# Attention layers of a graph-transformer kernel: head products from half-precision parts stacked over the partitions, squared lengths from token-major rows

## The reference

```python
def softmax_kernel(data, proj, is_query, eps=0.0001):
    d = data.shape[-1]
    normalizer = d ** (-0.25)
    ratio = proj.shape[0] ** (-0.5)
    data_dash = jnp.einsum('bhnd,md->bhnm', data * normalizer, proj)
    diag = jnp.sum(data ** 2, axis=-1, keepdims=True) * 0.5 * normalizer ** 2
    if is_query:
        m = jnp.max(data_dash, axis=-1, keepdims=True)
    else:
        m = jnp.max(data_dash, axis=(-2, -1), keepdims=True)
    return ratio * (jnp.exp(data_dash - diag - m) + eps)
...
for i in range(DEPTH):                      # DEPTH = 2
    y = layernorm(x, ln1_g[i], ln1_b[i])
    q = (y @ Wq[i] + bq[i]).reshape(B, N, HEADS, DIM_HEAD).transpose(0, 2, 1, 3)
    k = (y @ Wk[i] + bk[i]).reshape(B, N, HEADS, DIM_HEAD).transpose(0, 2, 1, 3)
    v = (y @ Wv[i] + bv[i]).reshape(B, N, HEADS, DIM_HEAD).transpose(0, 2, 1, 3)
    qp = softmax_kernel(q, proj[i], True)
    kp = softmax_kernel(k, proj[i], False)
    k_sum = kp.sum(axis=2)
    d_inv = 1.0 / jnp.einsum('bhnm,bhm->bhn', qp, k_sum)
    ctx = jnp.einsum('bhnm,bhnd->bhmd', kp, v)
    o = jnp.einsum('bhmd,bhnm,bhn->bhnd', ctx, qp, d_inv)
    x = x + o.transpose(0, 2, 1, 3).reshape(B, N, INNER) @ Wo[i] + bo[i]
    y = layernorm(x, ln2_g[i], ln2_b[i])
    x = x + gelu(y @ W1[i] + b1[i]) @ W2[i] + b2[i]
```

## Time and profile before

| what | value |
|---|---|
| three runs | 3261.3, 3269.97 and 3289.47 us; median 3269.97 |
| profiled execution | span 3276.7 us; no other time of it is given |
| TensorE busy | 2823.4 us (86%) |
| VectorE busy | 1606.1 us (49%) |
| ScalarE busy | 1067.3 us (33%) |
| GpSimd busy | 1172.1 us (36%) |
| TensorE's mean granted clock | 0.911 of full speed |

### The profile page before, as it was taken

One profiled execution on the slowest core, in us unless ns is written; L12 is line 12 of the kernel. 1 busy time (PEld: TensorE's weight loads), 2 busy tenths in 40 slices (PEclk: granted clock), 3 DMA queues, 4 the chain that ended last, 5 costly groups with the idle time before them and its releaser, 6 DMA issues. The chain is left out here.

```text
span 3276.7 us, 45967 instructions
## 1 busy us (share of the span) xinstructions
PE 2823.4 (86%) x16963; PEld 1813.0 (55%) x16963; DVE 1606.1 (49%) x3306; ACT 1067.3 (33%) x2420; POOL 1172.1 (36%) x1445
## 2 busy tenths in 40 slices
PE   7897999899899989979995974999789969579774
PEld 4554577465566746545553553777446646345453
DVE  8763537733553763366634535222245366551543
ACT  3243236423323642321313321444232225320132
POOL 2030677566367757833122221111003216400042
PEclk9998899899889989988997996999899969889897
DMA  2001345333144533331010003999801039700097
GB/s 61 1 26 49 116 151 159 118 103 103 36 122 149 164 104 112 120 94 37 15 33 26 26 20 121 416 415 414 302 15 40 20 144 333 233 21 0 32 349 266
DMA packets 163938, 415.33 MB, mean 127 GB/s; under 512 B 23931, under 2 KB 75675, under 8 KB 140236
## 3 DMA queue, kind: packets, MB, share of 16 engines
q1 hardware_dynamic: 149213, 362.10, 32.6%
q0 software_dynamic: 12960, 42.48, 3.4%
q10 hardware_dynamic: 1555, 7.95, 1.0%
HBM read 325.37 MB, written 87.09 MB: 126 GB/s over the span
## 5 line engine op out<-in xcount | busy, mean ns | idle before, releaser
L2436 POOL TENSOR_SCALAR raw<-raw 128x512 f32<-128x512 f32 x380 | 261.2, 687 | 1203.4 <-PE ps L447 521.7
L461 PE MATMUL ps<-units,ARENA 128*125 128x512 f16 x2880 | 635.8, 383 | 12.3 <-DVE ARENA L1652 5.3
L447 PE MATMUL ps<-ARENA,units 128*128 128x500 f16 (+1 forms) x2952 | 535.9, 344 | 6.1 <-ACT ARENA L1258 3.9
L461 PEld LDWEIGHTS ps<-units,ARENA 128*125 128x125 f16 x2880 | 390.0, 138 | 252.4 <-DVE X L2156 16.4
L447 PEld LDWEIGHTS ps<-ARENA,units 128*128 128x128 f16 x2952 | 289.4, 98 | 252.1 <-issue 19.1
L1639 DVE TENSOR_TENSOR ARENA<-tmp,ARENA 128x500 f16<-128x500 f32 (+3 forms) x289 | 194.1, 675 | 415.9 <-ACT ARENA L1258 238.8
L1257 ACT ACTIVATE tmp<-ps,cols 128x500 f32<-128x500 f32 (+1 forms) x204 | 131.8, 646 | 374.1 <-PE ps L447 367.3
L2440 POOL TENSOR_TENSOR AT<-raw,AT 128x512 f16<-128x512 f32 x200 | 234.9, 1175 | 17.0
L415 PE MATMUL ps<-ident,ARENA 125*128 125x125 f32 x440 | 92.1, 364 | 165.8 <-ACT ARENA L1258 48.6
L2440 POOL TENSOR_TENSOR units<-raw,units 128x512 f16<-128x512 f32 x180 | 220.0, 1222 | 15.3
L2484 POOL DMA_INDIRECT ARENA<-rows_d,proj x81 | 80.6, 995 | 393.8 <-DVE ARENA L1964 367.8
(11 more groups left out here) (435 smaller groups left out, 4355.0 us busy)
## 6 DMA issues: line engine op xcount, KB each, us to landing
ARENA<-split_d SPq DMA_DIRECT2D x135, 1024.0 KB, 10.3
raw<-in_moe SPq DMA_DIRECT2D x200, 256.0 KB, 3.0
split_d<-AT SPq DMA_DIRECT2D x200, 256.0 KB, 2.5
raw<-in_units SPq DMA_DIRECT2D x180, 256.0 KB, 2.6
ARENA<-split_d SPq DMA_DIRECT2D x27, 1280.0 KB, 8.9
...
```

Source lines behind the costliest of these rows:

```text
L447: ins = pe.matmul(o[:, 0:nt * R], wt, mv_, start=(i == 0), stop=(i == len(steps) - 1))
L461: ins = pe.matmul(o[0:R, :], th(srcT, h, k, t, 1), w(k, g), start=(i == 0), stop=(i == len(steps) - 1))
L2436: pool.tensor_scalar(r, r, WEIGHT_SCALE, 1.0, ALU.mult, ALU.mult).then_inc(sem("pool_step"), 1)
```

## The change

- **Head products.** Each head's keys (then queries) are kept as two half-precision parts in one stack of 128 partitions (`stack`): the rounded value on 64 of them and the rest on the other 64. A product over all 128 partitions with a table that has the same 64 rows on both halves gives the sum of both parts. The table is itself split into two half-precision parts (`features`), so a head takes two products of 256 columns and a pair four (L630 of the new program).
- **Their evictions.** `evac_heads` has three ScalarE operations for each of the twelve banks: the full value to a stage `tmp` in float32, 128 rows, and the rounded halves to the two heads' stacks, 64 rows each. `low_heads` adds two VectorE subtractions of 64 rows for each bank, which write the rests. The stages are three, so ScalarE also waits for VectorE three banks behind.
- **Squared lengths.** `token_rows` brings the keys or queries to token-major form on TensorE: for each tile eight products of 64 columns with a table `sum_halves` (two identities, one on top of the other), one bank for each tile. ScalarE squares the bank with a scale (`square_rows`, 125 x 512, three buffers), and VectorE sums each head's 64 squares (`square_sums`). The float32 products with `sel`, the table and `copy_diag` are gone.
- **Order and waits.** For keys, TensorE's pass for the squared lengths still stands behind the value projection, for queries behind the query projection. It now waits for the twelve rests (`lo_T`). `low_heads` stands on VectorE ahead of the value rows for keys and behind the last combining steps of the key loop for queries.
- **Once.** `proj` is loaded without being zeroed first, both halves of its 256 columns in the same place; VectorE scales it and makes the two half-precision parts (five operations in place of one). The memsets of `sel` are replaced by one addition.
- **Adjacency loops.** They count from 0 to the number of groups; TensorE reads two registers per tile in place of three, and VectorE still three.

```diff
--- before.py
+++ after.py
...
+NORM_SCALE = (0.5 * float(DH) ** -0.5) ** 0.5
...
-        sel = sb("sel", [128, KC, HEADS])
+        sum_halves = sb("sum_halves", [128, DH], F16)
...
+        def stack(h, t0, nt, p0=0, p1=128):
+
+            return halves["K"][p0:p1, h * N + t0 * R:h * N + (t0 + nt) * R]
+
+        def features(dep, part):
+
+            return proj[:, dep, NBF + part * NBF // 2:NBF + (part + 1) * NBF // 2].bitcast(F16)
+
...
+        key_squares = [Q[0:R, 3200 + i * D:3200 + (i + 1) * D] for i in range(3)]
+        query_squares = [Y[0:R, i * D:(i + 1) * D] for i in range(3)]
...
-                first = pe.value_load(span_i[0][:, dt:dt + 1], min_val=0, max_val=GROUPS - 1)
-                end = pe.value_load(span_i[1][:, dt:dt + 1], min_val=1, max_val=GROUPS)
-                before = pe.value_load(span_i[2][:, dt:dt + 1], min_val=-GROUPS, max_val=T * GROUPS)
-                with pe.Fori(first, end) as it:
+                groups = pe.value_load(span_i[1][:, dt:dt + 1], min_val=1, max_val=GROUPS)
+                before = pe.value_load(span_i[2][:, dt:dt + 1], min_val=0, max_val=T * GROUPS)
+                with pe.Fori(0, groups) as it:
...
 
-            def head_pair(buf, t, hp, o):
-
-                return pe.matmul(o[0:R, :], tr(buf, hp, t, 1), proj[:, dep, :], start=True, stop=True)
-
-            def row_norms(sq):
-
-                pe.wait_ge(sem("sqT"), s.more("sqT", 12))
-                pe.wait_ge(*left("dve"))
-                o = bank("dve", "read_dve")
+            def head_pair(t, hp, o):
+
+                for h2 in range(2):
+                    for part in range(2):
+                        ins = pe.matmul(o[0:R, h2 * NBF:(h2 + 1) * NBF], stack(2 * hp + h2, t, 1), features(dep, part),
+                                        start=(part == 0), stop=(part == 1))
+                return ins
+
+            def token_rows():
+
                 for t in range(T):
-                    for c in range(KC):
-                        ins = pe.matmul(o[0:R, t * 8:t * 8 + 8], tr(sq, c, t, 1), sel[:, c, :], start=(c == 0), stop=(c == KC - 1))
-                ins.then_inc(sem("filled_dve"), 1)
+                    pe.wait_ge(*left("dve"))
+                    o = bank("dve", "squares_of")
+                    for h in range(HEADS):
+                        ins = pe.matmul(o[0:R, h * DH:(h + 1) * DH], stack(h, t, 1), sum_halves[:, :], start=True, stop=True)
+                    ins.then_inc(sem("filled_dve"), 1)
 
...
-                gemm_T([(w, "YT", 4)], "kT")
...
-                row_norms(Q)
...
-                pe.wait_ge(sem("kT"), s.more("kT", 12))
+                pe.wait_ge(sem("lo_T"), s.more("lo_T", 12))
+                marks[f"key_rows{dep}"] = len(given["dve"])
+                token_rows()
...
                         pe.wait_ge(*left("act"))
-                        head_pair(K, i % T, i // T, bank("act", "kp")).then_inc(sem("filled_act"), 1)
+                        head_pair(i % T, i // T, bank("act", "kp")).then_inc(sem("filled_act"), 1)
...
-                gemm_T([(w, "YT", 0)], "qT")
...
-                row_norms(Y)
-                pe.wait_ge(sem("qT"), s.more("qT", 12))
+                pe.wait_ge(sem("lo_T"), s.more("lo_T", 12))
+                marks[f"query_rows{dep}"] = len(given["dve"])
+                token_rows()
...
-            def evac_square(dst, sq, name, bias):
+            def evac_heads(bias):
 
                 for k, (t0, nt) in STEPS["k"]:
+                    i = len(lo_signal)
                     act.wait_ge(sem("filled_act"), s.more("filled_act"))
                     o = s.bank("act")
-                    act.activation(tr(sq, k, t0, nt), o[:, 0:nt * R], ACT.Square, bias=bias(k), scale=WS).then_inc(sem("sqT"), s.one("sqT"))
-                    act.activation(tr(dst, k, t0, nt), o[:, 0:nt * R], ACT.Identity, bias=bias(k), scale=WS).then_inc(sem(name), s.one(name))
+                    if i >= STAGES:
+                        act.wait_ge(sem("lo_T"), lo_signal[i - STAGES])
+                    act.activation(tmp[:, i % STAGES, 0:nt * R], o[:, 0:nt * R], ACT.Identity, bias=bias(k), scale=WS)
+                    for h2 in range(2):
+                        a, b = h2 * DH, (h2 + 1) * DH
+                        ins = act.activation(stack(2 * k + h2, t0, nt, a, b), o[a:b, 0:nt * R], ACT.Identity, bias=bias(k)[a:b, :], scale=WS)
+                    ins.then_inc(sem("heads"), s.one("heads"))
+                    lo_total[0] += 1
+                    lo_signal.append(lo_total[0])
+
+            def square_rows(slots):
+
+                for t in range(T):
+                    if t >= 3:
+                        act.wait_ge(sem("squares_read"), s.seen["squares_read"] - 2)
+                    act.wait_ge(sem("filled_dve"), s.more("filled_dve"))
+                    act.activation(slots[t % 3], s.bank("dve")[0:R, :], ACT.Square, scale=NORM_SCALE).then_inc(sem("squares_of"), s.one("squares_of"))
+                    s.more("squares_read")
...
-                evac_square(K, Q, "kT", lambda k: col(f"L0bk{dep}", k))
+                evac_heads(lambda k: col(f"L0bk{dep}", k))
+                s.seen["filled_dve"] = marks[f"key_rows{dep}"]
+                square_rows(key_squares)
...
-                evac_square(K, Y, "qT", lambda k: col(f"L0bq{dep}", k))
+                evac_heads(lambda k: col(f"L0bq{dep}", k))
+                s.seen["filled_dve"] = marks[f"query_rows{dep}"]
+                square_rows(query_squares)
...
-                before = dve.value_load(span_i[2][:, dt:dt + 1], min_val=-GROUPS, max_val=T * GROUPS)
-                with dve.Fori(first, end) as it:
...
-            dve.memset(proj[:, :, :], 0.0).then_inc(sem("proj_zero"), s.one("proj_zero"))
-            dve.memset(sel[:, :, :], 0.0).then_inc(sem("dve_step"), s.one("dve_step"))
-            dve.wait_ge(*s.latest())
-            for c in range(KC):
-                dve.memset(sel[0:64, c, 2 * c:2 * c + 1], 0.5 * float(DH) ** -0.5)
-                ins = dve.memset(sel[64:128, c, 2 * c + 1:2 * c + 2], 0.5 * float(DH) ** -0.5)
-            ins.then_inc(sem("tables"), s.one("tables"))
+            dve.wait_ge(sem("ident"), 1)
+            tt(sum_halves[:, :], ident[:, 0:DH], ident[:, DH:128], ALU.add).then_inc(sem("tables"), s.one("tables"))
...
             dve.wait_ge(sem("proj_loaded"), s.more("proj_loaded", 64))
-            ts(proj[:, :, :], proj[:, :, :], float(DH) ** -0.25, None, ALU.mult).then_inc(sem("proj_scaled"), s.one("proj_scaled"))
-
-            def copy_diag():
-                dve.wait_ge(sem("filled_dve"), s.more("filled_dve"))
-                o = s.bank("dve")
-                dve.tensor_copy(diag[0:R, :], o[0:R, 0:T * 8]).then_inc(sem("read_dve"), s.one("read_dve"))
+            then(ts(proj[:, :, 0:NBF], proj[:, :, 0:NBF], float(DH) ** -0.25, None, ALU.mult))
+            for dep in range(2):
+                then(dve.tensor_copy(features(dep, 0), proj[:, dep, 0:NBF]))
+                ins = tt(features(dep, 1), proj[:, dep, 0:NBF], features(dep, 0), ALU.subtract)
+            ins.then_inc(sem("proj_scaled"), s.one("proj_scaled"))
+
+            def low_heads(k, t0, nt):
+
+                dve.wait_ge(sem("heads"), s.more("heads"))
+                wide = tmp[:, staged[0] % STAGES, 0:nt * R]
+                tt(stack(2 * k, t0, nt, DH, 128), wide[0:DH], stack(2 * k, t0, nt, 0, DH), ALU.subtract)
+                tt(stack(2 * k + 1, t0, nt, 0, DH), wide[DH:128], stack(2 * k + 1, t0, nt, DH, 128), ALU.subtract).then_inc(sem("lo_T"), s.one("lo_T"))
+                staged[0] += 1
+
+            def square_sums(slots):
+
+                for t in range(T):
+                    s.more("filled_dve")
+                    dve.wait_ge(sem("squares_of"), s.more("squares_of"))
+                    dve.tensor_reduce(diag[0:R, t * HEADS:(t + 1) * HEADS], slots[t % 3].rearrange("p (h c) -> p h c", c=DH), AX_X, ALU.add)\
+                        .then_inc(sem("squares_read"), s.one("squares_read"))
...
+                for k in range(KC):
+                    for t0, nt in CH:
+                        low_heads(k, t0, nt)
...
-                copy_diag()
+                square_sums(key_squares)
...
-                copy_diag()
+                for k in range(KC):
+                    for t0, nt in CH:
+                        low_heads(k, t0, nt)
+                square_sums(query_squares)
...
                 if u == 1:
-                    sp.wait_ge(sem("proj_zero"), 1)
                     for dep in range(2):
                         for h2 in range(2):
-                            sp.dma_start(proj[h2 * DH:(h2 + 1) * DH, dep, h2 * NBF:(h2 + 1) * NBF],
-                                         proj_in[dep]).then_inc(sem("proj_loaded"), 16)
+                            sp.dma_start(proj[h2 * DH:(h2 + 1) * DH, dep, 0:NBF], proj_in[dep]).then_inc(sem("proj_loaded"), 16)
```

19 lines of the change are left out of this document (12 added, 7 removed).

## The result

The changed kernel takes 3241.89 us (median of 18 runs, 3218.09 to 3264.57) against 3273.59 of the kernel before in the same comparison (18 runs, 3258.68 to 3300.98). The ratio is 0.9891, 95% interval 0.9868 to 0.9914: 1.1% faster, some 36 us by the ratio; the two medians lie 31.7 us apart. The forecast was 3216, or 54 us. The profiled execution spans 3258.8 us, 17.9 less than the profiled one before; its own time of 3261.49 lies near the upper end of the changed kernel's 18. A second profile of the same program, taken later, spans 3236.4, and the difference between these two turned out to be the heart of the case.

A forecast was written before the change was run, and what follows sets the result against it. With TensorE's share cut, VectorE was taken to bound the query loop. Per layer 10 + 7 + 7 + 3.5 = 27.5 us, two layers 55, less 1.3: 53.7, so 3216 against the median; range 3187 to 3250.

The forecast's parts named there:

- Faster by over 1%: Whole kernel: a time below 3237 us, chance 0.75.
- Query loop: Query loop of each layer: an item falls from 2.16 to 1.91 us, 10 us gained over 40 items.
- VectorE's 1.91 is then the largest: Query loop item: VectorE needs 1.91 us, more than TensorE's 1.75 and ScalarE's about 1.5, so it sets the pace.
- TensorE still bounds: Rival, both layers: VectorE's stalls shrink and its queue stays full; 41 us gained a layer, 3190; chance 0.12.
- The head product itself: Head products on TensorE: four half-precision products take 0.44 us against 0.853, leaving 1.75 per query item.
- Key loop: Key loop of each layer: 7 us gained, between 0 and 14, 5 in the steady part and 2 in the first.
- Clock: Rival: TensorE, waiting for VectorE between short products, gets 1.2 GHz in the loops; priced on query items, 3340; chance 0.06.
- Squared lengths of the keys: Keys' pass of each layer: 16.5 us down to 8.7 or 10.9 by clock, 7 us gained.
- Query pass: Queries' squared lengths: 15.8 us less 9.5, less 2.8 for the longer eviction chain and GpSimd: 3.5 us gained a layer.
- Once only: Ahead of the first layer norm: five operations for L1808's one lose 1.3 us; adjacency loops 0, between -1 and +1.
- GpSimd: Weight staging ends at 608.9; second feed-forward unit ready at 620, wanted at 636.6: no wait. Rival of lateness: 3238, chance 0.05.
- Evictions under the projections: Projections: TensorE's 25.5 us for 12 banks cover ScalarE's 20.4 and VectorE's 21.2, except the queries' last evictions.

The follow-up runs named there:

- all_fill: Changed kernel plus unread products after items 2 to 13 of each key loop and 36 ahead of the query pass's wait: 3214.27 us, ratio 0.9832.
- border_fill: Changed kernel plus unread products at the key loop's start, ahead of the query pass, and at TensorE's waits in the key loop's steady part: 3199.41 us, ratio 0.9763.
- double_heads: Changed kernel with every head product of both loops made twice into its own bank: 3239.19 us (median of four), ratio 0.9889.
- extra_load: Changed kernel with one more register load per tile on TensorE in the adjacency loops, as before the change: last tile starts at 158.19 us.

## Why the prediction was right, and where it was wrong

The direction and the range 3187 to 3250 held. "Faster by over 1%" held by the ratio, narrowly (its interval reaches 0.9914); the bound in us that I had put to it, 3237, did not, nor did the forecast's own range, 3202 to 3232. The likeliest time of 3216 was 26 us too low, and its sum is right only by parts: that the time fell into the range is in part luck, since gains that I had counted too small stood against a loss that I had not counted. By my own list, a granted clock below 1 in the loops was to show me wrong, and it was there.

- **Query loop (forecast 10 a layer, measured 16.6 and 17.9).** The step that failed is "VectorE's 1.91 is then the largest". I had added its rows up with the gaps between them (1.66) and put the mean stall of L1881 on top. In the running loop the shortest distance between two reduces was 1.38 us, for short instructions overlap (L1938 starts 0.08 us after L1933 at 529.01). The stall stayed as it was (L1933 means 0.390), so by estimate VectorE needs 1.38 + 0.23 = 1.61, less than TensorE's 1.69. TensorE bounds the loop at 1.69, as the rival "TensorE still bounds" had it (I gave it 16 a layer and 0.12).
- **The head product itself (forecast 0.44 in place of 0.853, the item on TensorE 1.75).** Right, a little low in gain: an item is 1.69, or 0.47 less; doubled, 0.44 more.
- **Key loop (forecast 7 a layer, measured -22.3 and -18.3, in eight loops a mean of -16).** This is the term that failed most. At full clock it was near: the shortest loop seen is 80.2 us, 8.3 under the old one, and those of all_fill and border_fill take 82 to 85. What came in between is the rival *Clock*, in the loop that I had not priced it for. I gave it 0.06 because a stretch with 2.33 of 5.00 us busy stood at 1.00. That row says that 2.67 us of waiting in 5 did not lower the clock there; it doesn't say what does. The experiments show that the time of the old float32 head products, 0.853 us of each item, was what held the clock up: with the same time filled by new products it is 0.96 and 1.00 again (double_heads), without it there are stretches at 0.50 in every plain loop, up to nearly the whole of it.
- **Squared lengths of the keys (forecast 7, measured 9.3 and 9.5).** Right and low: the pass ran at 1.00 and took 4.9 us for 80 products, 0.061 each, near the 0.058 that I took from the earlier trace rows. VectorE's ten sums took 6.0 us where I had 7.3, and its first reduce came 7.3 us after the projection, not 8.7.
- **Query pass (forecast 3.5, measured 0.1 and -2.1 with the projection before it, 1.7 in layer 1 by VectorE's first reduce).** The wait of "some 3 us" was 4.47. Behind it the pass ran at half clock, 8.5 us on TensorE and 10.2 to VectorE's first reduce, where I had taken 9.5, between its values for the two clocks. The projection ahead lost 1.1 and 2.3 us to the half clock of the key loop, which I had not counted. With filler the stage is 4.2 and 2.0 us shorter than in the kernel before (all_fill), near the 3.5.
- **Once only (forecast 1.3 lost).** The five operations lost 1.2, as counted. What stands ahead, put at 0 between -1 and +1, gained 5.0; 0.6 of it is the start of the program, and the register load on TensorE is the rest (the last tile is 4.6 us later in extra_load).
- **GpSimd.** Staging ended at 614.3, where I had 608.9 from the trace of before; the second feed-forward unit was first used at 656.23 and nothing waited for it.
- **Evictions under the projections.** They cost nothing: TensorE's 53.3 and 53.6 us for the projections of keys and values are no longer than before, and in the query projection it is busy throughout.

By the ledger: 53.7 forecast, + 14.5 for the query loops, + 4.8 for the key passes, + 5.2 for what comes once, - 54.6 for the key loops (40.6 lost in place of 14 won), - 9.0 for the query passes, and + 3.3 in the rows that I had left at nothing, are 17.9. The median of the runs is better than this profile: its mean granted clock is 0.887, and 15 of the 18 have more, up to 0.901.

What stays open: why one execution keeps the full clock for most of a loop and the next does not, with the same instructions, and whether columns or idle time decide it.
